# One stage of four groups from the end of the first experts to the turned keys, with the projection's biases added by products

## What is computed

```python
# end of layer 0 (x: the stream; fused: the two selected experts' weighted sum)
inner = (r - mean(r)) * rsqrt(var(r) + LN_EPS) * ln_gamma + ln_beta    # r = x + fused
x = _layernorm(x + inner, axis=-1)                                     # outer
# attention of layer 1
qkv = x @ qkv_w + qkv_b                                                # [4096, 384]
q, k, v = jnp.split(qkv, 3, axis=-1)
q = q.reshape(Bx, SNx, HEADS, HD)                                      # 16 heads of 8
k = k.reshape(Bx, SNx, HEADS, HD)
q = q / (jnp.linalg.norm(q, axis=-1, keepdims=True) + 1e-06) * qn_scale + qn_bias
k = k / (jnp.linalg.norm(k, axis=-1, keepdims=True) + 1e-06) * kn_scale + kn_bias
# then two training steps on (k, v), and the output from q
```

## Time and profile before

| | us |
|---|---|
| median of three runs | 2276.35 |
| the profiled execution's own time | 2262.35 |
| its span (first to last instruction) | 2260.6 |
| TensorE / VectorE / ScalarE / GpSimd busy | 1848.0 / 1655.1 / 1195.1 / 579.1 |
| mean granted TensorE clock, share of 2.4 GHz | 0.906 |

### The profile page before, as it was taken

How to read it: one execution, slowest core, us unless ns; L and a number is a source line. 1 busy time by engine, 2 the same in 40 slices (tenths; PEclk the granted TensorE clock), 3 DMA queues, 4 the chain that set the end, 5 groups by cost and what they waited for, 6 DMA issues and landing times. The chain is left out here.

```text
span 2260.6 us, 35457 instructions
## 1 busy us (share of the span) xinstructions
PE 1848.0 (82%) x11436; PEld 1489.3 (66%) x11436; DVE 1655.1 (73%) x4042; ACT 1195.1 (53%) x2749; POOL 579.1 (26%) x620
## 2 busy tenths in 40 slices
PE   6999999999999999965791328999799988742771
PEld 4888888888888888853571326776677766622771
DVE  5999999999999999956666676776577755557433
ACT  5888888888888888843342313333233323231332
POOL 0111111111111111103466163432144401000472
PEclk9999999999999999966995668999899999965995
DMA  6000000000000000042641000000000000040343
GB/s 217 1 1 1 1 1 1 1 1 1 1 1 2 1 1 1 1 105 44 105 124 49 23 0 1 0 0 0 1 0 0 0 1 3 2 127 15 92 92 85
DMA packets 64585, 62.47 MB, mean 28 GB/s; under 512 B 10673, under 2 KB 54145, under 8 KB 64177
## 3 DMA queue, kind: packets, MB, share of 16 engines
q1 hardware_dynamic: 54048, 43.85, 6.6%
q0 software_dynamic: 10384, 16.72, 4.5%
HBM read 41.42 MB, written 18.86 MB: 27 GB/s over the span
## 5 line engine op out<-in xcount | busy, mean ns | idle before, releaser
L521 DVE TENSOR_TENSOR probT<-turn_ps,probT 128x512 fp32r<-128x512 f32 x512 | 335.1, 686 | 63.4 <-ACT probT L435 63.2
L450 ACT ACTIVATE prob<-prob,negmax 128x512 f32<-128x512 f32 x512 | 375.4, 740 | 4.5 <-DVE negmax L515 4.5
L269 POOL TENSOR_TENSOR x<-x,scaled 128x512 f32<-128x512 f32 x128 | 166.7, 1303 | 810.3 <-DVE scaled L536 810.3
L515 DVE CUSTOM_DVE_ANT_0 prob<-score_ps,bias 128x512 f32<-128x512 f32 x512 | 340.9, 684 | 6.7 <-issue 0.9
L435 ACT CAST probT<-turn_ps 128x512 fp32r<-128x512 f32 x512 | 283.9, 598 | 21.7 <-PE turn_ps L341 21.7
L341 PE MATMUL turn_ps<-ident,prob 128*128 128x128 f32 x2048 | 266.2, 273 | 1.3 <-DVE probT L521 1.1
L358 PE MATMUL work_ps<-probT,val 128*128 128x512 f32 x1024 | 257.1, 393 | 0.1
L341 PEld LDWEIGHTS turn_ps<-ident,prob 128*128 128x128 f32 x2048 | 236.7, 140 | 28.2 <-DVE probT L521 3.4
L329 PE MATMUL score_ps<-k,q 64*128 64x512 f32 x1536 | 212.9, 408 | 3.7 <-DVE negmax L515 2.3
L358 PEld LDWEIGHTS work_ps<-probT,val 128*128 128x128 f32 x1024 | 187.5, 188 | 39.8 <-DVE probT L521 1.7
L329 PEld LDWEIGHTS score_ps<-k,q 64*128 64x128 f32 x1536 | 134.9, 184 | 49.1 <-issue 19.7
(11 more groups left out here) (495 smaller groups left out, 4054.1 us busy)
## 6 DMA issues: line engine op xcount, KB each, us to landing
ew<-L_ffn_fc_weight SPq DMA_DIRECT2D x32, 256.0 KB, 3.5
bias<-bias_line SPq DMA_DIRECT2D x16, 448.0 KB, 10.5
mid_rows<-row SPq DMA_DIRECT2D x40, 128.5 KB, 3.2
last_rows<-row SPq DMA_DIRECT2D x40, 64.0 KB, 1.8
rows_dram<-rows SPq DMA_DIRECT2D x1, 2304.0 KB, 18.7
acc_dram<-zero POOLq DMA_DIRECT2D x1, 2112.0 KB, 16.7
acc<-acc_dram SPq DMA_DIRECT2D x4, 528.0 KB, 6.0
x_rows<-x SPq DMA_DIRECT2D x4, 512.0 KB, 8.0
```

The lines of the kernel that those rows point to most:

```text
L269: pool.tensor_tensor(mine, mine, scaled[a][:, :, :], ALU.add).then_inc(added, 1)
L450: act.activation(mine, mine, ACT.Exp, bias=negmax[p % 2][:, i, a:a + 1], scale=-1.0, accum_out=total[p % 4][:, i, a:a + 1]).then_inc(exp_d ...
L515: dve.tensor_tensor_reduce(prob[p % 2][a][:, i, :], score_ps[i % 2][a][:, :], bias[:, h, first:first + SEQ][:, ::-1], -1.0, 3.0e38, ALU.ad ...
L521: dve.tensor_tensor(probT[1][:, g % QT, :], turn_ps[g % 2][:, :], probT[0][:, g % QT, :].bitcast(F32), ALU.subtract).then_inc(turned_lo, 1)
```

## The change

`finish_0`, the load block, `transpose_tokens`, `qkv`, the block that turns `proj`, and the first call of `transpose_parts` are replaced by one block, `finish_and_project`. It has four groups of 8 tiles, staggered: in step s, group s is measured, group s-1 gets its inner normalisation, gamma and the sum, group s-2 its outer normalisation, and then `projected(s - 2)` takes the queries, keys, values and turned keys of that group, in pairs of tiles u. Both normalisations use `Norms`. The weights of queries and keys are also multiplied with the head scales, so that one product of 512 columns gives the plain and the scaled values; the biases come in by a second product with two rows (a high and a low part, fp32r). GpSimd adds the shifts. Tiles that layer 1 needs are allocated before layer 0's experts (`home_ttt`), and for the room `apart_sq` in `places_0` becomes bf16. The core of the diff:

```diff
-        minus_low, apart_sq = core.sb(st, "minus_low", [P, TILES]), core.sb(st, "apart_sq", [P, TILES, P])
+        minus_low, apart_sq = core.sb(st, "minus_low", [P, TILES]), core.sb(st, "apart_sq", [P, TILES, P], BF16)
...
-        finish_0(core, keep, gamma, beta)
+        finish_and_project(core, ins, keep, gamma, beta)
...
+        @block.gpsimd
+        def _(pool):
...
+            fetch(0)
+            pool.memset(tiny[:, :], 1e-6).then_inc(ones_ready, 1)
+            pool.memset(ones[:, :], 1.0).then_inc(ones_ready, 1)
+            pool.iota(halves[:, :], pattern=[[0, 1]], base=0, channel_multiplier=-1, allow_small_or_imprecise_dtypes=True).then_inc(ones_ready, 1)
+            pool.wait_ge(small_in, 64)
...
+            for g in range(1, GROUPS):
+                fetch(g)
+            pool.wait_ge(laid, 4)
+            for c in range(CHUNKS):
+                pool.wait_ge(unit, 4 * (c + 1))
+                shift_part(c, 1, k_shifted)
+                shift_part(c, 0, q_shifted)
...
+            def project(t):
+                c, mine = t // 4, slice(t % 4 * P, (t % 4 + 1) * P)
+                if t % 4 == 0:
+                    pe.wait_ge(xT_ready, c + 1)
+                if t >= 4:
+                    pe.wait_ge(unit, t - 3)
+                pe.matmul(qk_ps[t % 4][:, :], xT[c % 2][:, mine], w[:, 0:V_AT], start=True, stop=False)
+                pe.matmul(qk_ps[t % 4][:, :], ones_r[:, :], b_parts[:, 0:V_AT], start=False, stop=True).then_inc(qk_done, 1)
...
+                pe.matmul(v_ps[c % 2][:, mine], xT[c % 2][:, mine], w[:, V_AT:], start=True, stop=False)
+                mm = pe.matmul(v_ps[c % 2][:, mine], ones_r[:, :], b_parts[:, V_AT:], start=False, stop=True)
...
+            for c in range(CHUNKS):
+                turn_x(c)
+                for t in range(4 * c, 4 * c + 4):
+                    project(t)
...
+                if c >= 1:
+                    turn_k(c - 1)
+            turn_k(CHUNKS - 1)
...
+        @block.scalar
+            def projected(g):
+                for j in range(PER_GROUP + 2):
+                    u, c = PER_GROUP * g + j, 2 * g + j // 2
+                    if j < PER_GROUP:
+                        if j % 2 == 0:
+                            copy_x(c)
+                        squares(u)
+                    if 1 <= j <= PER_GROUP:
+                        root(u - 1)
+                    if j in (2, 4):
+                        copy_v(c - 1)
+                    if j == 1 and g >= 1:
+                        copy_k(2 * g - 1)
+                    if j == 5:
+                        copy_k(2 * g)
...
+                for k in range(G):
+                    if k == G // 2 and s >= 2:
+                        outer.root(act, s - 2)
+                    if s <= GROUPS:
+                        inside((s - 1) * G + k)
...
+                for k in range(G):
+                    if k == G // 2 and s < GROUPS:
+                        inner.root(act, s)
+                    if s >= 2:
+                        outside((s - 2) * G + k)
+                if s >= 2:
+                    projected(s - 2)
...
+        @block.vector
+            def projected(g):
+                for j in range(PER_GROUP + 2):
+                    u = PER_GROUP * g + j
+                    if j < PER_GROUP:
+                        measure(u)
+                    if 1 <= j <= PER_GROUP:
+                        divide(u - 1)
...
+            for s in range(GROUPS + 2):
+                if s < GROUPS:
+                    dve.wait_ge(fetched[s], 16 * G)
+                for k in range(G):
+                    if s < GROUPS:
+                        dve.bn_stats(inner.raw[:, s * G + k, :], f[:, s * G + k, :]).then_inc(inner.seen, 1)
+                    if s >= 2:
+                        outer.moments(dve, s - 2, k)
...
+                if 1 <= s <= GROUPS:
+                    shape(s - 1)
+                    dve.wait_ge(summed, s)
+                for k in range(G):
+                    if 1 <= s <= GROUPS:
+                        t = (s - 1) * G + k
+                        dve.bn_stats(outer.raw[:, t, :], f[:, t, :]).then_inc(outer.seen, 1)
+                    if s < GROUPS:
+                        inner.moments(dve, s, k)
+                if s >= 2:
+                    projected(s - 2)
+            rest_of_k(CHUNKS - 1)
```

More of the change, by code:

```diff
@@ L131 @@
 BIAS_W = SEQ + (SEQ // P - 1) * P
[L134 to L163, removed]
 def transpose_parts(core, src, parts, ident):
@@ L991, in _, with home_ttt @@
                 sp.wait_ge(sent[r], 16 * (GROUPS // ROW_RING))
-def finish_0(core, keep, gamma, beta):
+TTT_HEADS, HD = 16, 8
+HID = 512
+HC = HID // P
+def home_ttt(core, st, keep):
+    keep["gate"], keep["val"], keep["projT"] = (core.sb(st, n, [P, HID]) for n in ("gate", "valw", "projT"))
+    keep["proj"] = core.sb(st, "proj", [P, HC, D])
+    keep["qk"], keep["v"] = core.sb(st, "qk", [P, TILES, 2 * D]), core.sb(st, "v", [P, TILES, D])
+    keep["ones"] = core.sb(st, "ones", [P, P])
+    keep["k_parts"] = keep["q_parts"] = [core.sb(st, f"turned_{half}", [P, N_TOK], F32R) for half in ("hi", "lo")]
@@ new lines, in shift_part @@
+            def shift_part(c, part, done):
+                mine = qk[:, 4 * c:4 * c + 4, part * D:(part + 1) * D]
+                pool.tensor_tensor(mine, mine, shift[:, part * D:(part + 1) * D].unsqueeze(1).to_broadcast([P, 4, D]), ALU.add).then_inc(done, 1)
+            inner.constants(pool)
+            outer.constants(pool)
+            fetch(0)
+            pool.memset(tiny[:, :], 1e-6).then_inc(ones_ready, 1)
+            pool.memset(ones[:, :], 1.0).then_inc(ones_ready, 1)
+            pool.iota(halves[:, :], pattern=[[0, 1]], base=0, channel_multiplier=-1, allow_small_or_imprecise_dtypes=True).then_inc(ones_ready, 1)
@@ new lines, in _ @@
+            pool.wait_ge(small_in, 64)
+            for i, wide in enumerate((scale, shift, scale, shift)):
+                half = wide[:, (i // 2) * D:(i // 2 + 1) * D].rearrange("p (h d) -> p h d", d=HD)
+                pool.tensor_copy(half, small[:, i, :].unsqueeze(1).to_broadcast([P, TTT_HEADS, HD])).then_inc(laid, 1)
+            for g in range(1, GROUPS):
[5 more added lines that the diff above has]
+                shift_part(c, 0, q_shifted)
@@ new lines, in rest_of_k @@
+            def rest_of_k(c):
+                dve.wait_ge(k_hi, c + 1)
+                dve.tensor_tensor(turned[1][:, columns(c)], k_ps[:, :], turned[0][:, columns(c)].bitcast(F32), ALU.subtract).then_inc(k_lo, 1)
+            def projected(g):
[5 more added lines that the diff above has]
+                        divide(u - 1)
+                    if j == 1 and g >= 1:
+                        rest_of_k(2 * g - 1)
+                    if j == 5:
+                        rest_of_k(2 * g)
```

370 lines of the change are left out of this document (152 added, 218 removed).

## The result

Four runs of the changed kernel took 2337.46 to 2348.17 us, median 2343.23; four of the one before 2273.44 to 2280.02, median 2276.97. The ratio is 1.0296, with a 95% interval of 1.0279 to 1.0312: slower by 67 us by the ratio, where 2280 was forecast and 2300 was the range's upper end. The profiled execution took 2341.81 us, its span 2340.1.

What follows compares the result with a forecast made beforehand. It took VectorE, gathers and waits between engines to bound the replaced 161.8 us. 1245.6 + 86.4 + 23.0 + 3 + 3.4 + 1.8 = 1363.2 against 1359.3, 3.9 us later, gave 2276.4 + 3.9 = 2280; range 2267 to 2300.

Steps and rivals of the forecast that it cites:

- A, the first product: Stage's start to first product: group 2's gathers ready at 1235.9, then a chain of 9.7 us, first product at 1245.6.
- B, the groups: Products of four groups of four pairs: 21.6 us each, 86.4 in all, with half clock for 4.6 us at each start.
- C and ports, between the groups: Last product of a group to first of the next: 10.4, 6.8 and 5.8 us, plus 3 for GpSimd and VectorE sharing ports.
- D and the phase's end: After the last group: last shift, transposes, copy and subtraction 3.4 us, then 1.8 until ScalarE's first cast.
- The ring: Waits inside a group that take one pair at a time: 4.9 us per pair, TensorE busy 2.8 and idle 2.1.
- Rival (a): Clock falls inside groups from TensorE's 2.1 us idle per ring: 2300 with half the pairs hit, 2316 with all; chance 0.22.
- (b): Ports (7.5 us instead of 3), handoffs and short bias product cost their upper bounds: +13 us, 2289; chance 0.14.
- (c): Clock does not fall between groups, and instructions overlap a little more: 8 us faster, 2268; chance 0.17.
- the clock in the middle of groups is 0.5: One of the signs named in advance that would show the forecast wrong: TensorE at half clock inside the groups.

Runs made afterwards that it cites:

- the three runs with a lead-in of 44.7 us: Changed kernel with biases first in fp32 (1.0313), biases of 64 rows (1.0274), or 128 rows with norms between pairs (0.9981); ratios against the kernel before.

## Why the prediction was wrong

The forecast's 165.6 us of stage against the measured 232.1, by its own steps:

- **A, the first product**: 48.0 us after the stage's start forecast, 49.8 measured. That it came so near was in part luck, for two errors nearly cancelled. Group 2's gathers were there after 35.0 us, not 38.3, since a gather took 1.25 us instead of 1.33 and the eighth was issued 10.9 us after the start instead of 13.1. And the chain from there to the first product, forecast at 9.7, took 14.8, with VectorE standing still three times (1.42, 2.12 and 2.41 us):

```profile
1240.69 0.29 DVE L1235 BATCH_NORM_STATS2 norm_raw<-f 128x6 f32<-128x128 f32 x1 [3.86 <-DMA f<-last_rows,home]
...
1247.73 1.23 DVE L1190 TENSOR_TENSOR f<-f,x 128x1024 f32<-128x1024 f32 x1 [2.12 <-remote]
...
1252.66 0.17 DVE L571 SCALAR_TENSOR_TENSOR norm_square<-norm_apart 128x8 f32<-128x8 f32 x1 [2.41 <-remote]
```

"remote" marks a wait whose releaser the profile does not show. In the three runs with a lead-in of 44.7 us these stops are absent and the chain takes 9.7 us, as forecast. What causes them is open.
- **B, the groups**: 4 x 21.6 = 86.4 forecast. Measured from first product to the last unit product: 36.2 for the first and 37.1 for each of the other three, 147.6 in all. This term alone is 61 of the 66.5 us by which the stage was missed.
- **C and ports, between the groups**: 23 + 3 = 26 forecast; from the last unit product to the next group's first product 11.7, 8.4 and 7.5, 27.6 in all. Near, but the ports cost more than was taken. Beside GpSimd's two shifts of 1.26 us each the moments `norm_sums` and `norm_apart` took 0.66 and 1.09 us in the first gap, instead of 0.15 each:

```profile
1291.81 2.48 POOL L1035 TENSOR_TENSOR qk<-qk,shift 128x512 f32<-128x512 f32 x2 [7.45 <-DVE qk L1202]
...
1292.45 0.66 DVE L564 TENSOR_TENSOR norm_sums<-norm_raw 128x8 f32<-128x8 f32 x1
...
1293.23 1.09 DVE L566 TENSOR_TENSOR norm_apart<-norm_raw 128x8 f32<-128x8 f32 x1
```

The first shift ends at 1293.07 and the second at 1294.29, the two moments at 1293.11 and 1294.32: each waited for the whole rest of the shift beside it, as the prediction's rule of the Trainium skill on the two sides of SBUF has it. That is 1.5 us here and 1.8 in each of the other gaps (0.86 and 1.23 instead of 0.15 each), 5.0 in all against the 3 taken and the 7.5 of the upper bound. The rest of C came to 22.6, against 23.
- **D and the phase's end**: 3.4 + 1.8 forecast, 3.9 + 3.3 measured (first cast 3.3 us after the last subtraction). The phase's end was 1.5 us longer than forecast.

Two readings in the working are loose, without weight for the result: the 32.0 us for 24 gathers run from the issue of the 8th to that of the 32nd, not from the landing at 1213.2, and the terms that end a group (0.4, 0.65, 1.1 and 1.68) add up to 3.8 us and not to 3.7.

**The step that failed** is in B: "The bias product of 512 columns is 0.23 from start to start". That row is a product of 128 rows between products of 128 rows. In the kernel the bias product has 2, and the price of a product is not its columns alone when its neighbours use another number of rows. With it failed the premise that TensorE runs at full clock 4.6 us into each group; in the changed kernel it never did. The ring itself was right to 0.04 us: with zero rows added it took 4.86 us and the four groups 86.4.

What stood in its place has two parts. The changes of rows make a tile 1.02 us longer at half clock (3.85 against 2.83) and 0.73 at full clock (2.15 against 1.42), 0.18 to 0.26 us for each of the four changes. Over 32 tiles that is at most 23 us at full clock, since a part would fall into the ring's idle time. The other 38 or more of the 61 us come with the clock at 0.50; that split is arithmetic, not a run of its own, but the run with 128 rows removes both together and gives 57 us back.

A rule of the Trainium skill would have pointed there ("TensorEngine Tiling (Array Packing)", section "Key Properties"): changing the tiling mode of the array drains it. The page does not say that a product of fewer rows counts as another mode, and gives no price. The weight loads at 1261.34 and 1262.06 behave as if it did, and 64 rows cost as much as 2; the 0.18 to 0.26 us are this case's.

**Rival (a)**, the clock falling inside the groups, was the nearest, with 0.22, but its mechanism was not what happened. It blamed the ring's idle time of 2.1 us, and in the run with 128 rows the clock stayed at 0.99 through both such times of the first group (1.45 and 1.83 us). It also priced a ring at half clock at 7.4 us; measured were 1281.45 - 1272.69 = 8.76, because its tiles lacked the pauses. So even the worst case of that rival, 2316, lay 27 us under the result. The rule of the Trainium skill that was cited beside it ("TensorE: Matmul & The Clock Gate", section "A second HAM failure mode: psum-queue depth-cycling") is not borne out inside these groups: the banks cycle in the same way in both runs, and in the one with 128 rows the clock stayed up. Rivals (b) and (c): the ports cost 5.0 us, between the 3 taken and the bound of (b), and the clock did fall in every gap, also in the run with 128 rows, in which it rose in the groups.

Of the signs named, "the clock in the middle of groups is 0.5" was the one that came true; first product, gaps and ring (in the run with 128 rows) were as announced. That there was no gain to be had without a better order also held: with no bias product at all the stage took 161.2 us, as long as before. The gain lay in the order of the pairs and norms.

Left open: how much of the low clock is due to the pauses and how much to the two-row columns in the changed kernel itself. Each was shown to lower it in a kernel of its own, but not their shares.

## What to carry to other kernels

Price a product on TensorE by its rows as well as by its columns: one of 2 or of 64 rows between products of 128 rows stopped the overlap of weight loads on both sides here. Adding zero rows to reach 128 gave back 57 of 67 us; where that is impossible, put the narrow products together (1.0131 instead of 1.0296). And look at the granted clock where PE shows full: busy time does not tell a dense engine from one that drains between instructions. When work is staggered over few PSUM banks, let the instructions that free a bank stand directly behind the ones that read it first, in every queue: with the transposes one pair earlier, that order was worth 20 us of stage (0.9981 to 0.9917 by the ratios). And when a sum comes out near the measured time, compare its steps too: step A was near by two errors that cancelled.

## What the runs showed of the hardware that I had not expected

- A change between 128 rows and 2 or 64 rows costs 0.18 us at full and 0.26 us at half clock, on average over both directions (four changes to a tile: 0.73 and 1.02 us; 64 rows were seen at half clock only), and about as much where all products are fp32.
- In the changed kernel the granted clock stayed at 0.50 over all four groups, with TensorE counted as busy for 33.12 of 36.40 us in the first.
- With the biases first and all products in fp32 the clock fell behind a stretch of two-row products from 1251.5 to 1253.8 us during which, and for 4 us after which, TensorE was never idle.
- In the run with bias products of 128 rows it stayed at 0.99 over 17.1 us in which TensorE was busy for only 10.89.
- A VectorE instruction on [128, 8] with two operands in SBUF took 0.66 to 1.23 us instead of 0.15 when it began beside a GpSimd shift, and ended within 0.04 us of that shift.
